# Attention band of an audio tower kernel: skewed when it is written to DRAM instead of when it is read back

## The reference, cut to what matters

```
z = tanh(conv2(x, W_z)); f = sigmoid(conv2(x, W_f)); o = sigmoid(conv2(x, W_o))   # 374 tokens
c[t] = f*c[t-1] + (1-f)*z;   h = o*c
y = layernorm(h); q, k, v = split(y @ W_qkv)            # 8 heads of 16
s[t, j] = q[t] . (k[t - off_j] * (1 + se_j)) / 4 + bias_j        # 39 offsets: 0..32, 48, 64, 96, 128, 192, 256
a = softmax_j(s);  out[t] = sum_j a[t, j] * v[t - off_j]
h = h + (out * gain * sigmoid(y @ W_gate)) @ W_out + b_out
h = h + router_top2(layernorm(h)) * ffn(layernorm(h))   # one shared FFN of width 512, 64 experts with room for 128 each
```

## Time and profile before

| | us |
|---|---|
| three timed runs | 446.92, 446.39, 444.70; median 446.39 |
| profiled execution, its own time | 446.38 |
| its span (first to last instruction of the core) | 444.6 |
| TensorE / VectorE / GpSimd / ScalarE busy in it | 419.7 / 391.5 / 373.5 / 318.7 |
| moved by DMA | 55.29 MB, mean 124 GB/s |

### The profile page before, as it was taken

The page is one execution under the profiler, slowest core; times in us unless marked ns, Lnnn a source line. Parts: engine busy times, 40 slices in busy tenths (PEclk is TensorE's granted clock), DMA queues, the critical chain, the costliest instruction groups (busy, mean ns, idle before and its releaser), DMA issues.

```text
span 444.6 us, 12613 instructions
## 1 busy us (share of the span) xinstructions
PE 419.7 (94%) x4554; PEld 283.2 (64%) x4554; DVE 391.5 (88%) x889; ACT 318.7 (72%) x648; POOL 373.5 (84%) x389
## 2 busy tenths in 40 slices
PE   8697798999999999999999999999999999998884
PEld 5354364776767576776767676776767676766763
DVE  2457999999999999999999999999999999997663
ACT  3664776867687787768687786768777777766764
POOL 8466999998998989898998989898998999995611
PEclk9979999999999999999999999999999999999999
DMA  6132467474645655473645646454655565556400
GB/s 231 34 84 42 120 163 170 116 166 119 142 106 129 156 139 137 94 173 90 150 115 140 156 125 140 104 137 124 140 125 126 122 158 135 140 138 150 101 11 26
DMA packets 77901, 55.29 MB, mean 124 GB/s; under 512 B 28272, under 2 KB 65168, under 8 KB 77712
## 3 DMA queue, kind: packets, MB, share of 16 engines
q1 hardware_dynamic: 77840, 54.49, 49.8%
HBM read 35.56 MB, written 18.92 MB: 123 GB/s over the span
## 4 chain that ended last, share of the span: by engine, by line
PE 60%; POOL 18%; issue 6%; DVE 5%; ACT 2%; POOLq 0%; ACTq 0%; DVEq 0%
PE bank L412 15%; PE bank L478 6%; POOL prod L1193 6%; PE bank L501 6%; PE bank L388 5%; PE bank L362 4%; PE bank L363 4%; PE bank L440 4%; POOL fprod L1178 4%; PE bank L428 3%; POOL near L1225 3%; PE bank L420 3%; POOL far L1211 2%; PE bank L396 2%; PE bank L455 2%
## 5 line engine op out<-in xcount | busy, mean ns | idle before, releaser
L1193 POOL TENSOR_TENSOR prod<-q,k 128x1496 f32<-128x1496 f32 x48 | 143.7, 3024 | 13.7 <-ACT q L645 9.6
L887 DVE SCALAR_TENSOR_TENSOR prod<-bank,par,k 128x1496 f32<-128x1496 f32 x80 | 141.0, 1765 | 5.1 <-ACT q L645 5.1
L412 PE MATMUL bank<-prod,ew 128*32 128x374 f32 x1024 | 87.4, 479 | 1.9 <-DVE mixin L840 1.9
L1178 POOL TENSOR_TENSOR fprod<-q,k 128x374 f32<-128x374 f32 (+6 forms) x112 | 80.1, 748 | 0.0
L412 PEld LDWEIGHTS bank<-prod,ew 128*32 128x32 f32 x1024 | 31.3, 109 | 46.4 <-issue 39.7
L585 ACT ACT_TABLE_LOAD x40 | 51.3, 1283 | 1.4 <-PEq L1325 0.7
L478 PE MATMUL bank<-x,par 128*128 128x374 f32 x128 | 49.9, 499 | 0.9 <-DVE near L934 0.7
L752 ACT ACTIVATE hid<-bank,par 128x374 f32<-128x374 f32 x64 | 36.2, 574 | 18.6 <-PE bank L478 17.6
L501 PE MATMUL bank<-par,hid 128*128 128x128 f32 x384 | 48.7, 278 | 0.5 <-ACT hid L752 0.5
L501 PEld LDWEIGHTS bank<-par,hid 128*128 128x128 f32 x384 | 45.2, 192 | 0.6 <-issue 0.6
L684 ACT ACTIVATE bandT<-bank 128x512 f32<-128x512 f32 x48 | 28.7, 599 | 18.3 <-PE bank L428 11.5
(11 more groups left out here) (119 smaller groups left out, 866.8 us busy)
## 6 DMA issues: line engine op xcount, KB each, us to landing
band_scratch<-attn SPq DMA_DIRECT2D x16, 769.5 KB, 5.3
band<-band_scratch SPq DMA_DIRECT2D x64, 192.0 KB, 3.8
vnear<-v_scratch SPq DMA_DIRECT2D x48, 192.0 KB, 2.8
v<-v_scratch SPq DMA_DIRECT2D x32, 192.0 KB, 4.3
v_scratch<-vtok SPq DMA_DIRECT2D x16, 192.0 KB, 4.1
xT<-x_dram SPq DMA_DIRECT2D x16, 187.5 KB, 4.3
vfar<-v_scratch SPq DMA_DIRECT2D x16, 128.0 KB, 4.2
out_dram<-osb SPq DMA_DIRECT2D x16, 128.0 KB
```

The source lines that it names most:

```text
L412: done = mm(home(f"s{c}")[32 * g:32 * g + 32, lo:N], ew[:, c * CW + j, :], src[:, j, lo:N], start=first or only, stop=last or only)
L887: v.scalar_tensor_tensor(bass.AP(prod[c][:, :, :].tensor, part * N, [[CW * N, 128], [PARTS * N, w], [1, N]]), home("q")[:, 0:N].unsqueeze( ...
L1178: last = g.tensor_tensor(fprod[:, i, o:N], q[q_.s][:, o:N], k[q_.s][:, KPAD:KPAD + N - o], ALU.mult)
L1193: g.tensor_tensor(bass.AP(prod[c][:, :, :].tensor, part * N, [[CW * N, 128], [PARTS * N, w], [1, N]]), q[q_.s][:, :].unsqueeze(1).broadcas ...
```

## The change: what it does, and the diff

`attn` and the DRAM scratch get rows of 512 numbers. `write_attn` now writes four strips of 32 partitions. In a strip, row r starts at r times 513 numbers, and its first 481 numbers (SPAN) are written, so the shift is made on the way out. `read_band` reads all of it with one transfer of 128 partitions, at pitch 512. The counts of the semaphores follow. Because the strips write only 481 of 512 numbers at shifting places, the rest of `band_scratch` must hold zeros: before the first turn, two transfers write the zeroed `attn` buffers (each 768 KB) over both halves of `band_scratch`, and the wait before `pipeline` covers them too. The order of the steps in `turn` stays on every engine.

```
+SPAN = BW - BT + 1
+BAND = NP * BW
-    band_dram = nc.dram_tensor("band_scratch", [2, NP, AW], fp32, kind="Internal").ap()
+    band_dram = nc.dram_tensor("band_scratch", [2, NP, BW], fp32, kind="Internal").ap()
-        attn = [sb(f"attn{s}", [128, TT, AW]) for s in range(2)]
+        attn = [sb(f"attn{s}", [128, TT, BW]) for s in range(2)]
+            def band_rows(q_):
+                return bass.AP(band_dram.tensor, q_.s * BAND, [[BW, 128], [128 * BW, TT], [1, BW]])
             def write_attn(q_):
                 sp.wait_ge(attn_ready, q_.b + 1)
-                after(sp, band_in[q_.s], 16 * BPT * q_.g)
-                rows = bass.AP(band_dram.tensor, q_.s * NP * AW, [[AW, 128], [128 * AW, TT], [1, AW]])
-                sp.dma_start(rows, attn[q_.s][:, :, :]).then_inc(band_out[q_.s], 16)
+                after(sp, band_in[q_.s], 16 * q_.g)
+                for u in range(BPT):
+                    rows = bass.AP(band_dram.tensor, q_.s * BAND + u * BT * BW, [[AW, BT], [128 * BW, TT], [1, SPAN]])
+                    sp.dma_start(rows, attn[q_.s][u * BT:(u + 1) * BT, :, 0:SPAN]).then_inc(band_out[q_.s], 16)
             def read_band(q_):
-                sp.wait_ge(band_out[q_.s], 16 * (q_.g + 1))
+                sp.wait_ge(band_out[q_.s], 16 * BPT * (q_.g + 1))
                 after(sp, bandT_mm[2], q_.b)
-                for u in range(BPT):
-                    block = bass.AP(band_dram.tensor, q_.s * NP * AW + u * BT * AW, [[BW, BT], [128 * AW, TT], [1, BW]])
-                    sp.dma_start(band[u * BT:(u + 1) * BT, :, :], block).then_inc(band_in[q_.s], 16)
+                sp.dma_start(band[:, :, :], band_rows(q_)).then_inc(band_in[q_.s], 16)
...
             for s in range(2):
                 sp.dma_start(v_dram[s, 0:FPAD, :], ...).then_inc(scratch_zero, 16)
-            sp.wait_ge(scratch_zero, 32)
+                sp.dma_start(band_rows(seq[s]), attn[s][:, :, :]).then_inc(scratch_zero, 16)
+            sp.wait_ge(scratch_zero, 64)
...
-                    pe.wait_ge(band_in[q_.s], 16 * BPT * (q_.g + 1))
+                    pe.wait_ge(band_in[q_.s], 16 * (q_.g + 1))
...
-                after(act, band_out[q_.s], 16 * q_.g)
+                after(act, band_out[q_.s], 16 * BPT * q_.g)
```

## The result

| | before | changed |
|---|---|---|
| median of 13 runs, us | 446.43 (444.57 to 448.50) | 448.99 (447.21 to 450.42) |
| profiled execution, own time / span | 446.38 / 444.6 | 447.34 / 445.6 |

The changed kernel is slower by a ratio of 1.0064 (95% interval 1.0045 to 1.0082), that is 2.6 us. The side was forecast, the size (453.1, range from 448.8) was not: the measured loss is 0.4 of the forecast one.

A forecast was written before the change was run, and what follows sets the result against it. TensorE was taken as the bound, busy for all 25.20 us of a middle turn. 446.38 + 5.0 (late x of sequence 2) + 1.7 (low clock) + 0 (strips and read) = 453.1 us; range 448.8 to 456.0.

The forecast's parts named there:

- Bound, and cost of the strips: Steady turns: TensorE bounds, never waiting for the band; strips 6.5 us, single read 5, cost 0.
- The chain z, f, `turn_h`, q, first product: Pipeline start: late x of sequence 2 delays TensorE's z and everything behind it, GpSimd's first product included; +5.0 us.
- Rival (c): First turns, between 14 and 26: idle gaps of TensorE and GpSimd swallow the delay; 446.4 us, chance 0.06.
- Value: the traffic of both in a row, 9.3 + 2 x 3.4 + 1.2: Before the first turn: both zeroing writes' traffic adds up; 17.3, less some overlap, so landed at 17.0.
- my reason for adding the tail: Zeroing writes: DMA busy share stays near 1 in a band write's tail, so both writes' 3.4 us were added.
- The clock, "+1.7": Pipeline start: after a 5.1 us TensorE gap, z, f and `turn_h` start at 1.2 GHz; +1.7 us.
- Rival (a): Startup zeroing writes flow fast, landing at 14.6, with no clock cost; +2.6, 449.0 us, chance 0.19.
- The formula that stands beside it: Startup zeroing writes: 2 us + bytes/436e3, an estimate of 5.6 us for both, landing at 14.7.

The follow-up runs named there:

- zero_late: Changed kernel with its two zeroing writes moved behind the load of x of sequence 3; 446.56 us, ratio 1.0003 to the kernel before.
- zero_twice: Changed kernel plus two more 768 KB startup writes to spare DRAM, rows of 512 at pitch 512, in the same wait; 454.25 us, ratio 1.0180.
- zero_512_at_513: Kernel before plus two startup writes, rows of 512 numbers at pitch 513; 455.74 us in one run.
- zero_513: Kernel before plus two startup writes in its own band write's shape, rows of 513 numbers at pitch 513; 457.17 us in one run.
- zero_pitch528: Kernel before plus two startup writes to spare DRAM, rows of 512 numbers at pitch 528 (2112 bytes); 448.86 us in one run.

## Why the prediction was right in its side and wrong in its size

- *Bound, and cost of the strips: right.* The middle turns and TensorE's order came out as said, no matmul waited for the band, and zero_late puts strips and read at 1.0003 (0.9974 to 1.0031). The terms inside were off without effect: 4.6 us for the strips where I took 6.5, 5.0 for the read, as taken.
- *The chain z, f, `turn_h`, q, first product: right.* The shift is +2.30 at z, +2.33 at `turn_h`, +2.32 at the first product, and +2.30 at the first band. Rival (c), that the first turns swallow it, is dead by the test that it named, GpSimd's first product.
- *"Value: the traffic of both in a row, 9.3 + 2 x 3.4 + 1.2": wrong.* This is the step that failed. Each write cost about 2.05 us of traffic where I had 3.4 (4.1 for a pair, as the second pair of zero_twice shows), the landing was at 14.17 for 17.0, the shift +2.3 for +5.0. I took the 3.4 from the band write of the trace, and did not see that its rows start 2052 bytes apart while those of the zeroing writes start 2048 apart. The sum itself fits that shape: at pitch 513 SP left the wait at 17.31 and 18.75. But my reason for adding the tail, a busy share near 1, was a misreading: from 49.0 to 51.0 the share is 1.67, 0.70, 0.64 and 0.38.
- *The clock, "+1.7": did not arise in the trace.* It hung on a gap of 5.1 us; with 2.57 the clock stayed up in the profiled run. Where the gap was as long as forecast or longer, the term measured 1.5 (zero_twice), 2.3 (zero_512_at_513) and 2.5 (zero_513). In zero_pitch528, with a gap of 2.22 us, it fell all the same (z to `turn_h` 4.31 us), so at this length a run can go either way. That some of the timed runs of the changed kernel pay it would fit a median of +2.6 to +2.9 over a shift of 2.3; it was not shown. Among its 13 runs time does go with the mean granted clock: 447.34 to 448.37 us at 0.992, 449.07 to 450.42 at 0.984 and below. But the mean of the 13 clocks, 0.9875, is no lower than in the runs of the kernel before beside the experiments (0.986 to 0.988), and 0.3 us would be too little to show in it.
- *Rival (a) was what happened*: landing at 14.6, +2.6, 449.0, with 0.19. It had the writes flow fast and the clock stay up, and both are in the trace. The formula that stands beside it, from the Trainium skill ("SBUF — State Buffer", "The DMA setup-cost knee"), was nearer than my sum as well: 5.6 us for both writes, an estimate, and landing at 14.7, for 4.9 us from the last issue and 14.17 measured. I had rejected it because it was too short for the trace's write, which was slow for another reason. The range began at 448.8, and the median of 448.99 lies 0.2 us inside it; that is owed to the room left for rival (a), not to the terms of my sum, which had a loss of 6.7 us for a measured 2.6.

## What to carry to other kernels

Before the duration of a transfer is taken from a row for another one, compare their shapes, start addresses in DRAM included, not only bytes and partitions. A one-time step before a pipeline counts in full when the first sequence's chain runs through it; ask of every wait at the start what is queued behind it, and move work that is needed only later behind the loads that are needed now, as zero_late does. Room found in the middle turns says nothing on the first and last.

## What the runs showed of the hardware that I had not expected

- A write of 128 partitions x 3 rows of 2 KB to DRAM: at a pitch of 2052 bytes a pair took 8.0 and 9.5 us from the second issue, at 2048 bytes 4.9, 5.4 and 5.7 us, at 2080 and 2112 bytes 4.9 us each. By these pairs the 4 bytes of padding that made the skew on the way back cost such a write 1.2 to 2.3 us, an estimate, hidden in this kernel. No single write at a pitch of 2048 bytes was measured.
- With one or more writes of 768 KB outstanding one issue on SP took 1.0 to 1.3 us (9.26 to 10.24 in the changed kernel's start, 11.64 to 12.95 in zero_twice), where the first issues there take 0.34 to 0.43. The cause was not tested.
- Seven matmuls on zeros in a gap of 3.8 us kept the granted clock at 1.00 and gave 1.4 us back (keep_warm, 0.9944 to 0.9988 of the time before).
